# Query transposes in an attention block: VectorE 32x32 blocks and SBUF-to-SBUF copies in place of TensorE transposes

## What is computed

```python
def _phi(u, omega):                       # feature map, M = 128
    proj = jnp.einsum('bhsk,mk->bhsm', u, omega)
    sq = 0.5 * jnp.sum(u * u, axis=-1, keepdims=True)
    stab = jnp.max(proj, axis=-1, keepdims=True)
    return jnp.exp(proj - sq - stab) / jnp.sqrt(m) + 1e-06

def _performer_attn(x, wq, wk, wv, wo, omega):
    ...
    pq = _phi(q * scale, omega)
    pk = _phi(k * scale, omega)
    kv = jnp.einsum('bhsm,bhsk->bhmk', pk, v)
    num = jnp.einsum('bhsm,bhmk->bhsk', pq, kv)
    den = jnp.einsum('bhsm,bhm->bhs', pq, jnp.sum(pk, axis=2))
    return (num / den[..., None]).transpose(0, 2, 1, 3).reshape(...) @ wo

xn = _layernorm(x)
x = x + attn_and_ffn(xn, ...) + gated_mix(xn, W_r, W_k, W_v, mu_r, mu_k)
```

## Time and profile before

| what | value |
|---|---|
| median of 3 runs | 3483.64 us (3478.65 to 3487.95) |
| profiled execution, first to last instruction | 3482.2 us |
| granted TensorE clock, mean | 0.993 of full |
| TensorE busy | 3422.0 us (98%), 29993 matmuls |
| VectorE busy | 2468.2 us (71%) |
| ScalarE busy | 1969.8 us (57%) |
| GpSimd busy | 1105.2 us (32%) |
| attend loop in the span | about 962 to 2046 us |

### The profile page before, as it was taken

How to read it: one execution, slowest core, us unless ns; L and a number is a source line. 1 busy time by engine, 2 the same in 40 slices (tenths; PEclk the granted TensorE clock), 3 DMA queues, 4 the chain that set the end, 5 groups by cost and what they waited for, 6 DMA issues and landing times.

```text
span 3482.2 us, 77456 instructions
## 1 busy us (share of the span) xinstructions
PE 3422.0 (98%) x29993; PEld 3151.9 (91%) x29993; DVE 2468.2 (71%) x4839; ACT 1969.8 (57%) x4240; POOL 1105.2 (32%) x861
## 2 busy tenths in 40 slices
PE   8999999999899999999999999999999999999998
PEld 6888888888788888888888889999999999999998
DVE  6767777677667777677777766666666666666666
ACT  6777777777556666666656654444444444444443
POOL 3554554545345454555555532000000000000000
PEclk9999999999899999999999999999999999999999
DMA  3222222222323333232332346444444444444443
GB/s 128 80 77 74 95 77 83 77 74 77 107 79 114 106 102 115 82 126 94 102 109 93 111 144 206 147 148 148 147 146 146 146 146 146 146 146 146 146 147 126
DMA packets 195355, 409.83 MB, mean 118 GB/s; under 512 B 27440, under 2 KB 52528, under 8 KB 194992
## 3 DMA queue, kind: packets, MB, share of 16 engines
q1 hardware_dynamic: 194992, 404.89, 34.6%
HBM read 292.50 MB, written 112.33 MB: 116 GB/s over the span
## 4 chain that ended last, share of the span: by engine, by line
PE 70%; DVE 2%; ACT 1%; issue 0%; POOL 0%; DMA 0%; ACTq 0%; POOLq 0%; DVEq 0%
PE ffn_hidden L175 30%; PE attend_gated L175 20%; PE ffn_result L175 8%; PE attend_num L175 6%; PE attend_feat L1425 3%; PE attend_feat L1445 1%; PE ffn_turn L1910 1%; PE attend_turn L1415 1%; DVE attend_kvz_lo L1393 1%; DVE attend_pT_lo L1354 1%; PE attend_feat L1452 1%; PE attend_turn L1434 0%; ACT attend_kvz_hi L1300 0%; DVE attend_kvz_lo L1396 0%; DMA ffn_r_in<-in_L_attn_w_dram 0%
## 5 line engine op out<-in xcount | busy, mean ns | idle before, releaser
L175 PE MATMUL ffn_hidden<-ffn_yT_hi,ffn_wa_hi 128*128 128x256 f32 x2048 | 574.1, 280 | 3.5 <-DVE ffn_wa_lo L1798 1.8
L175 PE MATMUL ffn_hidden<-ffn_yT_lo,ffn_wa_hi 128*128 128x256 f32 x2048 | 573.3, 280 | 0.0
L175 PE MATMUL ffn_hidden<-ffn_yT_hi,ffn_wa_lo 128*128 128x256 f32 x2048 | 572.0, 279 | 0.0
L316 POOL TENSOR_TENSOR ffn_n_rstd<-ffn_n_base,ffn_n_power 128x2 f32<-128x2 f32 x32 | 27.5, 860 | 1300.1 <-DVE ffn_n_negmean L311 1300.1
L1780 ACT ACTIVATE ffn_ht_hi<-ffn_hs 128x512 fp32r<-128x512 f32 x248 | 156.4, 631 | 420.6 <-DVE ffn_hs L1827 420.6
L175 PEld LDWEIGHTS ffn_hidden<-ffn_yT_hi,ffn_wa_hi 128*128 128x128 f32 x2048 | 385.0, 188 | 4.4 <-DVE ffn_wa_lo L1798 2.3
L175 PEld LDWEIGHTS ffn_hidden<-ffn_yT_hi,ffn_wa_lo 128*128 128x128 f32 x2048 | 385.2, 188 | 0.0
L175 PEld LDWEIGHTS ffn_hidden<-ffn_yT_lo,ffn_wa_hi 128*128 128x128 f32 x2048 | 384.9, 188 | 0.2
L635 POOL TENSOR_TENSOR keys_z_sum<-keys_z_sum,keys_e 128x512 f32<-128x512 f32 x192 | 259.6, 1369 | 232.9 <-ACT keys_e L703 232.9
L1831 DVE TENSOR_TENSOR ffn_ht_lo<-ffn_hs,ffn_ht_hi 128x512 fp32r<-128x512 f32 x248 | 173.6, 700 | 218.9 <-ACT ffn_ht_hi L1780 218.9
L1765 ACT ACTIVATE ffn_hid<-ffn_hidden,ffn_bias 128x256 f32<-128x256 f32 x496 | 206.1, 467 | 180.5 <-PE ffn_hidden L175 180.5
(11 more groups left out here) (305 smaller groups left out, 11669.3 us busy)
## 6 DMA issues: line engine op xcount, KB each, us to landing
ffn_tq<-part_d SPq DMA_DIRECT2D x248, 512.0 KB, 3.9
keys_xin<-in_L_attn_x_dram SPq DMA_DIRECT2D x32, 512.0 KB, 4.5
xn_d<-keys_xn SPq DMA_DIRECT2D x32, 512.0 KB, 3.0
xT_d<-keys_xT_whole SPq DMA_DIRECT2D x32, 512.0 KB, 2.6
u_d<-keys_uq SPq DMA_DIRECT2D x32, 512.0 KB, 3.1
shared_xTf<-xT_d SPq DMA_DIRECT2D x32, 512.0 KB, 6.0
shared_uq<-u_d SPq DMA_DIRECT2D x32, 512.0 KB, 4.9
r_d<-shared_gate SPq DMA_DIRECT2D x32, 512.0 KB, 3.1
```

The source lines that it names most:

```text
L175: last = pe.matmul(out, stationary[a], moving[b], start=start and n == 0, stop=stop and n == len(TERMS) - 1)
```

## The change

The queries are no longer turned by TensorE. VectorE transposes the 32x32 blocks of each loaded tile into a buffer `q_blocks` (new job `blocks`, two instructions of 128x512; `q_blocks` lies over `act_k20` and `act_k21`). Sixteen DMAs of 32 partitions by 1 KB bring the blocks to the right partitions (new job `cross` on SyncE); they write over `uq`, seen as `q_cross`. ScalarE and VectorE then split that into `qT.hi` and `qT.lo` (job `cross`), reading SBUF with a stride where they read PSUM before. Around this the lists are reordered: the squares of the next group move to the front of a body on ScalarE and VectorE, `sq` gets two buffers, the queries are loaded two groups ahead (job `load_q`, behind the split), and SyncE's `load_x` comes behind that load. `below` on TensorE waits for its own bank's last reader. Three waits elsewhere that named the TensorE transposes name the split.

```diff
         PE_BODY = [("max", 0, 0), ("num", 3, -1), ("k", 0, 0), ("max", 1, 0), ("k", 1, 0), ("r", 0, 0),
-                   ("below", 0, 0), ("feat", 0, 0), ("turn_q", 0, 1), ("r", 1, 0), ("out", 0, 0), ("feat", 1, 0),
-                   ("num", 0, 0), ("out", 1, 0), ("num", 1, 0), ("turn_q", 1, 1), ("wo", 0, -1), ("wo", 1, -1),
-                   ("num", 2, 0)]
-        DVE_BODY = [("top", 0, 0), ("top", 1, 0), ("recip", 0, -1), ("below", 0, 0), ("mix", 0, 1), ("kv", 0, 0),
-                    ("exp", 0, 0), ("o", 0, -1), ("out", 0, 0), ("sq", 0, 1), ("turn_q", 0, 1), ("sq", 1, 1),
-                    ("out", 1, 0), ("mix", 1, 1), ("hi", 1, 0), ("turn_q", 1, 1), ("wo", 0, -1), ("wo", 1, -1),
-                    ("stats", 0, -1),
+                   ("below", 0, 0), ("feat", 0, 0), ("r", 1, 0), ("out", 0, 0), ("feat", 1, 0),
+                   ("num", 0, 0), ("out", 1, 0), ("num", 1, 0), ("wo", 0, -1), ("wo", 1, -1), ("num", 2, 0)]
+        DVE_BODY = [("top", 0, 0), ("sq", 0, 1), ("top", 1, 0), ("sq", 1, 1), ("recip", 0, -1), ("below", 0, 0),
+                    ("mix", 0, 1), ("kv", 0, 0), ("exp", 0, 0), ("blocks", 0, 1), ("o", 0, -1), ("out", 0, 0),
+                    ("out", 1, 0), ("mix", 1, 1), ("hi", 1, 0), ("cross", 0, 1), ("cross", 1, 1), ("wo", 0, -1),
+                    ("wo", 1, -1), ("stats", 0, -1),
                    ("part_lo", 0, 0)]
-        ACT_BODY = [("num", 3, -1), ("norm", 0, -2), ("k", 0, 0), ("k", 1, 0), ("below", 0, 0), ("kv", 0, 0),
-                    ("r", 0, 0), ("exp", 0, 0), ("sq", 0, 1), ("mix", 0, 1), ("r", 1, 0), ("oT", 0, -1),
-                    ("num", 0, 0), ("turn_q", 0, 1), ("sq", 1, 1), ("exp", 1, 0), ("num", 1, 0), ("hi", 1, 0),
-                    ("turn_q", 1, 1), ("mix", 1, 1), ("num", 2, 0),
+        ACT_BODY = [("num", 3, -1), ("norm", 0, -2), ("sq", 0, 1), ("k", 0, 0), ("sq", 1, 1), ("k", 1, 0),
+                    ("below", 0, 0), ("kv", 0, 0), ("r", 0, 0), ("exp", 0, 0), ("mix", 0, 1), ("r", 1, 0),
+                    ("oT", 0, -1), ("num", 0, 0), ("exp", 1, 0), ("num", 1, 0), ("hi", 1, 0), ("cross", 0, 1),
+                    ("cross", 1, 1), ("mix", 1, 1), ("num", 2, 0),
                    ("part_hi", 0, 0)]
...
-                   ("rep_load", 0, -1), ("store_y", 0, -2), ("xb", 0, -1), ("store_r", 0, 0), ("sq", 1, 1),
-                   ("kv", 0, 0),
+                   ("rep_load", 0, -1), ("store_y", 0, -2), ("xb", 0, -1), ("cross", 0, 1), ("store_r", 0, 0),
+                   ("load_q", 0, 2), ("kv", 0, 0),
...
+        def from_cross(m):
+            return q_cross.rearrange("p i (c s) -> p c i s", s=KD)[:, 4 * m:4 * m + 4]
+        def in_tiles(part, m):
+            return part[:, 2 * m:2 * m + 2, :].rearrange("p c (t i s) -> p (c t) i s", t=TG, i=NC)
...
+                if job == "load_q":
+                    sp.wait_ge(q_split, 2 * g)
+                    wait_alone(sp, squared, TG * g, sp_passed)
+                    sp.dma_start(uq[:, :, :], u_g[g]).then_inc(q_loaded, 16)
+                if job == "cross":
+                    sp.wait_ge(blocks_made, g)
                     wait_alone(sp, squared, TG * g + TG, sp_passed)
+                    for i in range(NC):
+                        for j in range(NC):
+                            sp.dma_start(q_cross[j * KD:(j + 1) * KD, i, :], q_blocks[i * KD:(i + 1) * KD, j, :])\
+                                .then_inc(q_crossed, 16)
...
+                if job == "cross":
+                    act.wait_ge(q_crossed, 16 * NC * NC * g)
                     for j in range(HC):
                         wait(act, feat[j].full, 4 * g - 1 + n)
+                    act.activation(in_tiles(qT.hi, n), from_cross(n), ACT.Copy).then_inc(qT_hi, 1)
...
+                if job == "blocks":
+                    dve.wait_ge(q_loaded, 16 * g + 16)
+                    dve.wait_ge(ka_ready, 2 * g)
+                    for t in range(TG):
+                        last_blocks = dve.transpose(
+                            q_blocks[:, :, :].rearrange("p j (c t s) -> p t c j s", c=NC, t=TG)[:, t],
+                            uq[:, t, :].rearrange("p (c j r) -> p c j r", c=NC, j=NC))
+                    last_blocks.then_inc(blocks_made, 1)
+                if job == "cross":
                     dve.wait_ge(qT_hi, 2 * g + n + 1)
+                    dve.tensor_tensor(in_tiles(qT.lo, n), from_cross(n), f32(in_tiles(qT.hi, n)), ALU.subtract)\
+                        .then_inc(q_split, 1)
...
-                if job == "turn_q":
-                    pe.wait_ge(q_loaded, 16 * g + 16)
-                    wait(pe, q_split, 2 * g + n)
-                    ...
-                    last_turn.then_inc(q_turned, 1)
...
-                    pe.wait_ge(q_split, 2 * g + 2)
+                    pe.wait_ge(*((belowT_ready, g) if g else (q_split, 2)))
```

More of the change, by code:

```diff
@@ L35 @@
           ("omegaT_lo", 512), ("ident", 512), ("mu", 32))
-ATTEND_LATE = (("sq", 128), ("top", 128), ("below", 128), ("den", 128), ("rden", 128), ("mask", 32), ("n1_stats", 64),
+ATTEND_LATE = (("sq0", 128), ("sq1", 128), ("top", 128), ("below", 128), ("den", 128), ("rden", 128), ("mask", 32), ("n1_stats", 64),
                ("n1_mv", 32), ("n1_base", 32), ("n1_negmean", 32), ("n1_power", 32), ("n1_rstd", 32), ("n1_shift", 32),
@@ L998, in attend_pass @@
         act_k2 = [sb(f"act_k2{n}", [P, 2, GT]) for n in range(2)]
+        q_blocks = sb("q_blocks", [P, NC, GT])
+        q_cross = uq[:, :, :].rearrange("p t (h n) -> p (t h) n", h=2)
         ka = Pair(mem, ctx, "ka", [P, NC, GT])
         gate = sb("gate", [P, TG, D])
-        sq = sb("sq", [P, TG, NC, HC])
+        sq = [sb(f"sq{n}", [P, TG, NC, HC]) for n in range(2)]
         top = sb("top", [P, TG, NC, HC])
@@ L1109, in do @@
             def do(job, n, g, b, i):
-                if job == "sq" and n == 1:
-                    sp.wait_ge(q_turned, 2 * g + 2)
+                if job == "load_q":
[4 more added lines that the diff above has]
+                    sp.wait_ge(blocks_made, g)
                     wait_alone(sp, squared, TG * g + TG, sp_passed)
-                    if not (isinstance(g, int) and g == G - 1):
-                        sp.dma_start(uq[:, :, :], u_g[g + 1]).then_inc(q_loaded, 16)
+                    for i in range(NC):
+                        for j in range(NC):
+                            sp.dma_start(q_cross[j * KD:(j + 1) * KD, i, :], q_blocks[i * KD:(i + 1) * KD, j, :])\
+                                .then_inc(q_crossed, 16)
                 if job == "load_x":
@@ L1273, in do @@
                     wait(act, ka_ready, 2 * g + n - 1)
+                    wait(act, q_crossed, 16 * NC * NC * g)
                     act.activation(act_k2[n][:, :, :], halves(gated[n]), ACT.Relu).then_inc(k_free[n], 1)
@@ L1340, in do @@
                         dve.wait_ge(feat[j].free, 4 * g + 2)
-                    dve.scalar_tensor_tensor(out=below[:, :, :], in0=sq[:, :, :, :].rearrange("p t c h -> p t (c h)"),
+                    dve.scalar_tensor_tensor(out=below[:, :, :], in0=sq[g % 2][:, :, :, :].rearrange("p t c h -> p t (c h)"),
                                              scalar=-0.5, in1=top[:, :, :, :].rearrange("p t c h -> p t (c h)"),
@@ L1407, in do @@
             def do(job, n, g, b, i):
-                if job == "turn_q":
-                    pe.wait_ge(q_loaded, 16 * g + 16)
-                    wait(pe, q_split, 2 * g + n)
-                    if n == 0:
-                        wait(pe, belowT_ready, g)
-                    for c in range(2):
-                        for t in range(TG):
-                            last_turn = pe.transpose(turn[:, c * GT + t * P:c * GT + (t + 1) * P],
-                                                     uq[:, t, (2 * n + c) * P:(2 * n + c + 1) * P], ident[:, :])
-                    last_turn.then_inc(q_turned, 1)
                 if job == "max":
@@ L1501, in attend_pass @@
         left = AttendLeft(mix_full, mix_ready, carried, k_full[1], r_full[1], out_full[1], out_free, wo_full[1], wo_free,
-                          num.full, num.free, o_ready, squared, sq_ready, q_turned, q_split, belowT_ready,
+                          num.full, num.free, o_ready, squared, sq_ready, q_split, belowT_ready,
                           [f.full for f in feat], [f.free for f in feat], ka_ready, r_stored, y_stored, part_stored)
```

17 lines of the change are left out of this document (7 added, 10 removed).

## The result

The change makes the kernel slower: 3520.4 us median (3515.91 to 3523.21) against 3481.4 us (3478.65 to 3487.95) of the kernel before, ratio 1.0105 with a 95% interval of 1.009 to 1.0119. The kernel before has four runs here, one more than ahead of the prediction, where the median of three was 3483.64 us. The forecast was 3482 us, the range ended at 3515.

What follows compares the result with a forecast made beforehand. TensorE's order of work was taken to bound the attend loop; its saved 0.94 us a body become waits. Span 3482.2 - 1.8 (bodies) + 1.4 (median over span) = 3482 us, range 3470 to 3515.

Steps and rivals of the forecast that it cites:

- The bound: Attend loop: TensorE, busy 35.33 of 35.33 us in a body, sets the time by its order of work.
- What goes: TensorE loses two batches of four transposes per body: 0.94 us a body, 29.1 us over 31 bodies at most.
- The transposes and "o": VectorE's two transposes, 1.2 us, lie in a wait for mix_lo; "o" ends 0.40 us later; a body gains 0.02 us.
- the landing of the sixteen copies: SyncE issues them at 0.43 us each, landed by 1062.7; landing may slip to about 1066.0, 3.3 us of cover.
- Rival 2: Copies land after 1066.0, from about 0.65 us per issue, and "max" waits; 0.7 us gives 3511 us; chance 0.12.
- Rival 1: VectorE's transposes don't run under mix_lo, being excluded or slow: +28.6 us, 3512 us; chance 0.14.
- rival 3: TensorE's "wo" isn't held and the full 29.1 us come: 3454 us; chance 0.11 (all or part).
- Rival 4: The queries' load comes late and holds ScalarE's squares and "k": 31 us per us past cover, 3513 us; chance 0.03.
- The second reduce of squares: VectorE, now ahead of recip and below, 0.6 us; covered, as below_parts ends at 1043.55 and TensorE turns it at 1045.79.

Runs made afterwards that it cites:

- SyncE held: Changed kernel with sixteen copies issued, but the split waits for the first four alone; the other twelve go to room nobody reads: 3489.28 us, ratio 1.0018.
- the run without blocks: Changed kernel without the block transposes, but for one 32-column block of each, and without all copies but four small ones: 3484.06 us, ratio 1.0004.

## Why the prediction was wrong

**The bound** was right: TensorE's order sets the body, and where nothing keeps it waiting a body without the transposes takes 34.52 us. **What goes**: 0.94 us forecast, 0.81 us seen (35.33 to 34.52).

**The transposes and "o"** were right in mechanism and nearly in size. Two transposes 1.29 us (1.2 taken); both "o" end 2.3 us behind mix_lo; oT_lo ends 28.33 us after the start of "max" in body 10 with four copies (1309.85 + 2.39 - 1283.91) against 27.91 before, 0.42 later (0.40 forecast). The body gets 0.17 us longer, not 0.02: after a wait TensorE's second product of "wo" comes 0.34 us after the first (1312.30 to 1312.64), and I had taken 0.23. In first bodies of a batch the gain is 0.07 us (36.59 where the clock stays full), not 0.2. Without the copies' delay the forecast would have been 3482 against 3488 measured.

**The step that failed is the landing of the sixteen copies: 0.43 us an issue, set against the 3.3 us of cover of one normal body.** I took the broadcast loads' 0.43 us for an issue and put the two den stores' 0.65 us aside because they touch two partitions. The copies take 0.63 us, in all the forms that were tried: the den store was the nearer row, and its being different in shape was no reason. Sixteen times 0.20 us is 3.2 us, so the cover was gone, and a batch's first body has 1.3 us less of it: its transposes start 2.4 us later, and it is 1.1 us longer (with four copies).

**Rival 2 had the mechanism** (the copies' landing, from about 0.65 us per issue), with 0.12 where it should have been the forecast, and its arithmetic was short. By its own sum 0.63 us was the edge in a normal body (1053.6 + 16 x 0.63 + 2.3 = 1066.0), and the split starts 1.3 us behind the end of the issue (body 5), not 2.3; so body 7 is free of a loss: its split ended 0.6 us ahead of "max".

The loss came from what the sum left out. First, a batch's first body: transposes start 22.2 us into it instead of 19.8 because of the kv split, so sixteen issues end at 33.9 and the split at 37.1 (body 4, 37.16 us, against 36.59 with four copies). I had applied the test to a normal body alone. Second, single issues of up to 1.93 us: one in body 5 makes the sixteen 11.36 us. The trace of before has issues like that (of the queries' load, up to 1.64 us), and I had left them out. Third, a delay is not forgotten: behind the split VectorE has "wo", statistics and tops, GpSimd has diff behind the statistics, and so a body that follows a late one starts its transposes late as well (22.2 us in body 5). Body 15 (1477.27 to 1513.51, 36.24 us) shows this by itself, here on VectorE: its split ends 0.7 us ahead of the next "max", but the split of the body before ended right at its start, TensorE then waits 0.28 us for VectorE's tops, and the transposes come 20.5 us into the body instead of 19.8.

```profile
1476.53 0.69 DVE L1340 TENSOR_TENSOR shared_qT_lo<-shared_uq,shared_qT_hi 128x512 fp32r<-128x512 f32 x1
...
1497.80 1.29 DVE L1334 STREAM_TRANSPOSE attend_q_blocks<-shared_uq 128x512 f32<-128x512 f32 x2
...
1511.53 1.29 DVE L1340 TENSOR_TENSOR shared_qT_lo<-shared_uq,shared_qT_hi 128x512 fp32r<-128x512 f32 x2 [1.10 <-ACT shared_qT_hi L1252]
```

The 27 bodies lose 10.6 us in first, 12.1 us in second, 3.3 us in third and 3.5 us in fourth places; second bodies of a batch, no longer than others before, now lose most. Against the 36.59 and 35.50 us of the run with four copies they take 26.6 us more. In 12 of them the split's end sets the next "max", 0.06 us ahead of it: 20.1 us. In five (11, 15, 19, 23, 27) the split is in time and the body is longer by as much as its transposes start late: 2.5 us. Three (6, 12, 24) hold a stretch at half clock: 4.1 us; a fourth such body, 20, is among the twelve.

That this hangs on the landing is shown by the runs with twelve copies and with SyncE held, where ScalarE waits for copies 9.3 us in all and not at all, against 81.0 us; the 5.2 us that remain with four copies are the o chain's.

**Rival 1** fell (transposes run beside mix_lo), **rival 3** needed "o" ahead of mix_lo, as the prediction said, and came, with 0.81 us a body, in those bodies where mix_lo had been moved behind oT_lo and nothing else was late. **Rival 4** fell as it was put: SyncE's queue is held as long in the run with twelve copies to spare room, at no cost. Where the split itself is late, the load of xT behind it is late too, and GpSimd's diff waited for it seven times, 17.8 us in all; that is part of the third point. The second reduce of squares stayed covered in bodies in time; in late ones "below" waited for VectorE five times, 5.5 us, and whether the reduce has a part in it was not tested. The range took in rival 2 only up to 3515.

## What to carry to other kernels

Price a DMA that you have not seen by the dearest row with the same source memory (here the den store), and per instruction: sixteen small copies on one queue were sixteen times the issue, whatever their bytes, and fewer, larger transfers through DRAM were the quicker way here. Test a landing against its deadline in the latest body of the pattern and with one slow issue in it, not in the typical body; where an in-order engine stands behind the wait, count a miss there more than once. TensorE time that is saved counts only up to the next chain that was due at the same moment: here the o chain had 0.3 us of slack, and it paid only once two GpSimd instructions changed places, and only in the bodies where nothing else was late.

## What the runs showed of the hardware

TensorE's granted clock fell to half for short stretches in the loop, which never happened in these bodies before. After the change there are four: one stands behind the 1.59 us wait ahead of 1147.76 shown above, three in first bodies (12, 20, 24) behind waits for pT_lo. In the run without blocks there are five, all in first bodies; ahead of the one shown TensorE had waited twice for pT_lo, 0.22 us each, and was busy 2.36 of 2.80 us. The stretch after the change, then the one without blocks with its body:

```profile
1149.80:1153.20 3.40, 3.40 (x18) 3.40 (x17) 3.30 (x9) 1.44 (x3) 2.16 (x3) 0.51 0.75 269
```

```profile
1088.00:1090.80 2.80, 2.36 (x36) 1.95 (x36) 2.77 (x6) 0.00 (x0) 1.62 (x1) 0.97 0.82 272
1090.80:1094.00 3.20, 3.20 (x12) 2.82 (x12) 1.84 (x2) 2.01 (x4) 0.88 (x1) 0.50 0.05 8
1066.56:1104.29 37.73, 37.18 (x331) 32.02 (x330) 28.67 (x56) 22.86 (x46) 17.91 (x12) 0.95 0.33 115
```

These are 1.2 GHz instead of 2.4. In the run with four copies two first bodies hold such a stretch and take 37.74 us instead of 36.59, 1.15 us more; without blocks it is 37.73 instead of 36.21. Four at 1.15 to 1.5 us would be some 5 us of the 39, an estimate, and I had not counted that. What brings such a stretch is not shown. Bodies 24 and 28 of the run without blocks have the same two waits and keep the full clock, and so do all seven first bodies of the kernel before, whose only waits are these (in its 27 bodies: total, times, longest):

```profile
PE attend_feat L1445 <- DVE attend_pT_lo L1354: 3.0, 14, 0.2
```

A one-source instruction wasn't always free of GpSimd. The transposes ran beside mix_lo, but the cast of below_parts, one source too, took 1.26 us beside ka_lo (body 5 above) and takes 0.23 us alone. The Trainium skill, SBUF — State Buffer, section "Who interferes with whom", names copy and cast among those that can take the shared port pair; the 1.26 us agree with it.
